# GpSimd takes over the last layer norm's centring and gamma, and the planner's leads and grain change, in a four-layer graph network on one core

## Chip, core and metric

The kernel runs on one core of a Trainium2 chip. The metric is device time in microseconds (us) of one execution. The engines are named as in the profile: PE (TensorE, matrix products), DVE (VectorE), ACT (ScalarE), POOL (GpSimd) and SP (its queue issues the DMAs).

## What is computed

Inputs are 32 batches of 256 nodes with 256 features, and one adjacency matrix. Four layers follow one another, each on a layer-normed copy of x and each added to x:

```python
h = relu(layernorm(x)); x = x + gnn(h)              # layer 0: degree * (own product + b) + adj @ (h @ Wj)
h = relu(layernorm(x)); x = x + gat(h)              # layer 1: one attention head, masked softmax
h = relu(layernorm(x)); x = x + attention(h)        # layer 2: q, k, v, 8 heads, output product
h = relu(layernorm(x)); x = x + gat_ffn(h)          # layer 3: 4 GAT heads, elu, output GAT, elu, ffn
# the end of layer 3:
y = ffn + out
return (y - mean(y)) / sqrt(var(y) + eps) * ln_gamma + ln_beta
```

The change touches the last line. There mean and variance are those of a row of y, 256 elements.

## The kernel before

A batch lies in SBUF as 128 partitions by 2 chunks (`C = 2`) by 256. The work of a batch is cut into 267 named steps, each with an engine, a planned cost and the steps that it needs. Names that come back below, for layer 1: `amj` (the last product of layer 0, L966 `ps<-wp,at`), `x1` (its sum into x, L1283), `stats 1`, `aggr 1` (L1246, L1252: mean and variance), `inv_std 1` (POOL, L722 to L727), `rows 1` (ACT, L806 `tb<-xs`: the normed rows), `rows_T 1` (PE, L995 `ps<-ident,tb`: four transposes into columns), `rows_hi 1` and `rows_lo 1` (L814 on ACT and L1260 on DVE into `hT1`: a value is kept as a high and a low part for exact products), and `wh 0` (PE, L966 `ps<-w1g,hT`: layer 1's product, a first part of 4 matmuls with high parts and 8 more that need the low part).

For the 8 heads of layer 2: `scores` (PE, L1160, two heads at a time), `smin` (DVE, L1408: two instructions and two short read-outs for each head), `s_exp` (ACT, L919), `p_T` (PE, L995 `ps<-ident,pb`), `pT16_hi` (ACT, L927), `pT16_lo` (DVE, L1416) and `values` (PE, L1177). For layer 3: `attend` (PE, `ps<-pT,whs`), `elu_relu`, `elu_exp` (ACT, L888, L892), `elu` (DVE, L1380), `join` (PE, `ps<-wout,hid`), `tmin 5` (DVE, L1343 into `tbo`), `out_b2` (POOL, L785). The last norm: `y` (DVE, L1434), `stats 4`, `aggr 4`, `y_gamma` (DVE, L1439), `inv_std 4` (POOL, two instructions), `final` (DVE, L1449) and `store`.

The order of the steps on every engine is fixed while the program is built, by a list planner (`arrange`): it keeps a planned time for each engine and takes again and again the ready step with the earliest planned start, rounded to `GRAIN`; among those with the same rounded start it takes the one with the longest rest of work behind it. To this rest, `LEAD` adds a constant by the section of the step: layers 0 and 1, layer 2, the rest of layer 3, and the ffn with the last norm. On the chip each engine then runs its list strictly in that order and waits on semaphores. So an instruction whose operands are late holds back all that stands behind it on its engine. Work of four batches is interleaved.

```python
start, st = min(((max(free[st["engine"]], st["ready"]), st) for st in ready),
                key=lambda of: (round(of[0] / GRAIN), -of[1]["rest"]))
```

Of the kernel before, what the change touches and what calls it, by code (L numbers as in the profile page):

```python
# [5 lines left out]
def adj_preln_kernel(nc, x, adj, adj_t, L0_W_t, L0_b, L1_W, L1_a_src, L1_a_dst,  # L6
# [33 lines left out]
    with ctx:  # L40
# [3 lines left out]
        def sem(name):  # L44
            return ctx.enter_context(nc.semaphore(name))
# [468 lines left out]
        def ffn(a):  # L514
            transposed(a, TR_OUT, ("elu", GOUT))
            a("out_b2", 0, PO, 1.37, ("rows_T", TR_OUT))
            a("ffn1", 0, TE, 1.4, ("rows_lo", TR_OUT))
            a("f1_full", 0, SC, 0.75, ("ffn1", 0))
            a("f1_hi", 0, SC, 0.54, ("f1_full", 0))
            a("f1_lo", 0, PO, 1.25, ("f1_hi", 0))  # L520
            product(a, "ffn2", 0, (("f1_hi", 0),), (("f1_lo", 0),))
            a("y", 0, VE, 0.6, ("ffn2", 0), ("out_b2", 0))
            norm_chain(a, 4, ("y", 0))
            a("y_gamma", 0, VE, 0.8, ("aggr", 4))
            a("final", 0, VE, 0.8, ("y_gamma", 0), ("inv_std", 4), ("x_beta", 0))
            a("store", 0, SY, 0.05, ("final", 0))

# [51 lines left out]
            assert len(order) == len(todo)  # L579
            return order  # L580

        GRAIN, LEAD = 0.2, (34.0, 34.0, 33.0, 33.0)
        ISSUE = (0.07, 0.04, 0.05, 0.05, 0.05)

        SECTIONS = (("load", "x_deg", "mj", "mi", "mj_hi", "mj_lo", "x_mi", "amj", "x1", "x2"),
# [84 lines left out]
        wo_done, normalised = sem("wo_done"), sem("normalised")  # L670
        f1_done, f1_full, f1_hi, f1_lo, f2_done = (sem(n) for n in ("f1_done", "f1_full", "f1_hi", "f1_lo", "f2_done"))
        ob_ready, y_done = sem("ob_ready"), sem("y_done")
        vstep = sem("vstep")

        def batch(t, b):
            return t[b].rearrange("(c p) d -> p c d", p=P)
# [1 line left out]
        def run_steps(block, order):  # L678
# [32 lines left out]
            def _(pool):  # L711
# [59 lines left out]
                def normalise(p, u):  # L771
# [7 lines left out]
                    else:  # L779
                        last.then_inc(normalised, 1)  # L780

                def out_b2(_, u):
                    pool.wait_ge(rows_T[TR_OUT], u + 1)
                    for c in range(C):
                        last = pool.tensor_tensor(fu5[:, c, :], fu5[:, c, :], b2_b[:], ALU.add)  # L785
                    last.then_inc(ob_ready, 1)

                program = dict(inv_std=inverse_std, x_deg=x_deg, scale=scale, v_c=value_third, x_bo=x_bo, x_beta=x_beta, hid_lo=low_of_hidden, out_b2=out_b2, normal=normalise, f1_lo=low_of_ffn)
                for name, k, u in order:
                    if name in program:  # L790
                        program[name](k, u)
# [428 lines left out]
            def _(dve):  # L1220
# [3 lines left out]
                def mark(ins, key):  # L1224

                    count[0] += 1
                    ins.then_inc(vstep, 1)
                    marks[key] = count[0]
# [204 lines left out]
                    dve.wait_ge(ob_ready, u + 1)  # L1433
                    dve.tensor_tensor(fu5[:], fu5[:], bank(BJ), ALU.add).then_inc(y_done, 1)  # L1434

                def times_gamma(_, u):
                    dve.wait_ge(mv_ready[4], u + 1)
                    for c in range(C):
                        last = dve.scalar_tensor_tensor(out=fu5[:, c, :], in0=fu5[:, c, :], scalar=mv[4][:, c, 0:1],  # L1439
                                                        in1=gamma_b[:], op0=ALU.subtract, op1=ALU.mult)  # L1440
                    mark(last, ("yg",))

                def result(_, u):
                    dve.wait_ge(rstd_ready[4], u + 1)
                    after(("yg",))
                    dve.wait_ge(beta_ready, u + 1)
                    xu = xs[u % XB]
                    for c in range(C):
                        last = dve.scalar_tensor_tensor(out=xu[:, c, :], in0=fu5[:, c, :], scalar=rstd[4][:, c:c + 1],  # L1449
                                                        in1=xu[:, c, :], op0=ALU.mult, op1=ALU.add)  # L1450
                    last.then_inc(x_final, 1)
# [44 lines left out]
```

## Time and profile before

| | |
|---|---|
| median of 3 runs | 1876.4 us (1875.9 to 1878.53) |
| the profiled execution, its own time | 1877.61 us |
| its span, first to last instruction | 1875.7 us |
| busy PE, DVE, ACT, POOL | 1746.8, 1573.2, 1539.7, 862.1 us |
| mean granted clock | 0.98 |

The span leaves out 1.9 us that lie around the first and the last instruction. "Busy" is the time in which at least one instruction of the engine ran. A busy PE may still lose some time between its matmuls. Instructions of one engine overlap slightly, by about 80 ns on DVE, so distances between starts are used below, not durations.

### The profile page before, as it was taken

Reading aid. Unit: us, or ns where it says so; the run is one execution under the profiler, and the core shown is the slowest. Engines: PE = TensorE matmul, PEld = TensorE weight load, DVE = VectorE, ACT = ScalarE, POOL = GpSimd, SP = SyncE. Lnnn points to the kernel's source line nnn. Section 1 sums busy time; section 2 is a strip of 40 time slices with the busy share of each in tenths; the row PEclk is TensorE's granted clock in tenths of the full one; section 3 lists DMA queues with packets and bytes.
Section 4 is the critical chain, followed back from the end, with each engine's and each line's share of the span. In section 5 each row is a group of like instructions: output and inputs, shape, how many; then the busy total and the mean of one; then the engine's idle time right before and its main releaser. Section 6 shows DMA issues by size and latency. Waiting matters only on the chain. (4 is left out here: it accounts for less than half of the span.)

```text
span 1875.7 us, 45892 instructions
## 1 busy us (share of the span) xinstructions
PE 1746.8 (93%) x15880; PEld 1661.5 (89%) x15880; DVE 1573.2 (84%) x5359; ACT 1539.7 (82%) x3634; POOL 862.1 (46%) x1492
## 2 busy tenths in 40 slices
PE   0789999999999999999999999999999999999985
PEld 0678999999999999999999999999999999999874
DVE  6478988888889888888998888889888889988863
ACT  2368988888899888888988888898888889888872
POOL 4224544445554444555444445544444554443442
PEclk8799999999999999999999999999999999999997
DMA  5000000000000000000000000000000000000000
GB/s 165 12 24 2 20 23 19 24 25 24 13 24 19 19 24 24 24 13 24 19 23 19 24 24 21 16 19 24 18 24 24 13 24 19 24 13 19 18 18 12
DMA packets 31206, 43.83 MB, mean 23 GB/s; under 512 B 3328, under 2 KB 26880, under 8 KB 30976
## 3 DMA queue, kind: packets, MB, share of 16 engines
q1 hardware_dynamic: 30976, 40.91, 6.7%
q8 instruction: 127, 2.08, 0.5%
q14 instruction: 103, 0.84, 0.2%
HBM read 32.38 MB, written 8.52 MB: 22 GB/s over the span
## 5 line engine op out<-in xcount | busy, mean ns | idle before, releaser
L775 POOL TENSOR_TENSOR cx<-cx,rden 128x64 f32<-128x64 f32 x256 | 78.3, 327 | 511.8 <-DVE cx L1426 511.8
L919 ACT ACTIVATE pb<-lg,hmin 128x256 f32<-128x256 f32 x512 | 227.1, 499 | 42.3 <-DVE hmin L1408 39.8
L966 PE MATMUL ps<-wout,hid 128*128 128x256 f32 x1536 | 228.7, 290 | 1.8 <-ACT hid L933 1.0
L927 ACT ACTIVATE pT<-ps 128x512 f16<-128x512 f32 x256 | 145.5, 590 | 97.9 <-PE ps L1177 92.7
L1408 DVE CUSTOM_DVE_ANT_0 lg<-ps,maskp 128x256 f32<-128x256 f32 x512 | 190.9, 419 | 26.9 <-PE ps L1160 24.7
L966 PE MATMUL ps<-wh,hT 128*128 128x256 f32 x1536 | 212.4, 288 | 0.8 <-DVE whs L1324 0.8
L966 PE MATMUL ps<-pT,whs 128*128 128x256 f32 x1536 | 206.0, 283 | 3.0 <-DVE pT L1373 1.9
L966 PEld LDWEIGHTS ps<-wout,hid 128*128 128x128 f32 x1536 | 196.3, 190 | 9.9 <-ACT hid L933 1.4
L765 POOL TENSOR_TENSOR hid<-fu,hid 128x512 fp32r<-128x512 f32 x128 | 166.7, 1303 | 76.8 <-ACT hid L933 76.8
L966 PEld LDWEIGHTS ps<-pT,whs 128*128 128x128 f32 x1536 | 192.4, 191 | 4.2 <-DVE pT L1373 2.5
L966 PEld LDWEIGHTS ps<-wh,hT 128*128 128x128 f32 x1536 | 191.2, 190 | 3.9 <-DVE whs L1324 1.3
L1416 DVE TENSOR_TENSOR pT<-ps,pT 128x512 f16<-128x512 f32 x256 | 170.7, 686 | 10.1 <-ACT pT L927 8.9
L745 POOL TENSOR_SCALAR ea<-ea,rs 128x256 f32<-128x256 f32 x256 | 132.2, 530 | 86.0 <-DVE rs L1364 85.3
L863 ACT ACTIVATE ea<-tb,npeak 128x256 f32<-128x256 f32 x320 | 161.4, 507 | 0.1
L849 ACT ACTIVATE tb<-tb,cols 128x256 f32<-128x256 f32 x320 | 145.2, 508 | 18.7 <-DVE dmin L1343 18.7
L995 PE MATMUL ps<-ident,pb 128*128 128x128 f32 x1024 | 148.3, 275 | 5.1 <-ACT pb L919 4.5
L1380 DVE SCALAR_TENSOR_TENSOR fu<-rb,ps 128x512 f32<-128x512 f32 x160 | 108.8, 680 | 44.5 <-ACT rb L892 38.3
L1177 PE MATMUL ps<-v,pT 128*128 128x97 bf16 x2048 | 130.1, 208 | 10.0 <-DVE pT L1416 9.8
L1177 PEld LDWEIGHTS ps<-v,pT 128*128 128x128 f16 x2048 | 106.3, 98 | 24.8 <-DVE pT L1416 16.8
L1160 PE MATMUL ps<-kp,qp 32*128 32x256 f32 x1536 | 124.8, 294 | 2.3 <-DVE kp L1387 0.4
L995 PEld LDWEIGHTS ps<-ident,pb 128*128 128x128 f32 x1024 | 117.1, 141 | 9.0 <-ACT pb L919 8.5
L723 POOL TENSOR_TENSOR rstd<-ve,pow_half 128x2 f32<-128x2 f32 x160 | 117.4, 734 | 13.3
(188 smaller groups left out, 4790.0 us busy)
## 6 DMA issues: line engine op xcount, KB each, us to landing
tbc<-t_dram SPq DMA_DIRECT2D x32, 512.0 KB, 3.7
xin<-x_in SPq DMA_DIRECT2D x32, 256.0 KB, 2.7
out<-xs SPq DMA_DIRECT2D x32, 256.0 KB, 2.2
t_dram<-st_rows SPq DMA_DIRECT2D x128, 1.0 KB
xs<-a_heads SPq DMA_DIRECT2D x4, 128.0 KB, 5.5
pT<-a_heads SPq DMA_DIRECT2D x4, 128.0 KB, 4.5
lg<-W_out SPq DMA_DIRECT2D x2, 256.0 KB, 5.2
tb<-adj SPq DMA_DIRECT2D x1, 256.0 KB, 2.8
```

Source lines behind the costliest of these rows:

```text
L745: last = pool.tensor_scalar(ea(g)[:, c, :], ea(g)[:, c, :], rs[g][:, c:c + 1], 1.0, ALU.mult, ALU.mult)
L765: pool.tensor_tensor(hid[g % 2][:, 1], fu[:], f(hid[g % 2][:, 0]), ALU.subtract).then_inc(hid_lo, 1)
L849: last = act.activation(tb(g)[:, c, :], tb(g)[:, c, :], ACT.Prelu, bias=source_cols(g)[:, c:c + 1], scale=-1.0, alpha=SLOPE[g])
L863: act.activation(ea(g)[:, c, :], tb(g)[:, c, :], ACT.Exp, bias=npeak[g][:, c:c + 1], scale=1.0, accum_out=psums[g][:, c:c + 1]).then_inc(e ...
L919: last = act.activation(pb[h % 2][:, c, :], lg[h % 2][:, c, :], ACT.Exp, bias=hmin[h % 2][:, c:c + 1], scale=-1.0)
L927: act.activation(pT16[h % 2][:, 0], bank(head_bank(h)), ACT.Copy).then_inc(pT16_hi, 1)
L966: last = pe.matmul(dst, lhs(a, t), rhs(b, t), start=(not low and opens and n == 1), stop=(low is not False and closes and n == terms * len ...
L995: last = pe.transpose(bank(k)[:, kc, blk(c)], src[:, c, blk(kc)], ident[:])
L1160: last = pe.matmul(bank(head_bank(h))[:, c, :], qp[r, a, oc, blk(c)], kp[r, b, oc, :], start=(n == 0), stop=(n == 2))
L1177: last = pe.matmul(ps[:, at0:at0 + VC], pT16[h % 2][:, part, kc, blk(c)], v3[:, kc, h, :], start=(n == 0), stop=(n == 2 * C - 1))
L1408: last = dve.tensor_tensor_reduce(out=lg[h % 2][:, c, :], in0=bank(head_bank(h))[:, c, :], in1=maskp[:, c, :], scale=-SCALE, scalar=3.0e38 ...
L1416: dve.tensor_tensor(pT16[h % 2][:, 1], bank(head_bank(h)), pT16[h % 2][:, 0], ALU.subtract)\
```

## The change

`y_gamma` moves from DVE, where it is two instructions (subtract the mean, times gamma), to POOL, where it is four: two that subtract the mean, each waited for by its own semaphore, and two that multiply by gamma. `final` on DVE now waits for a semaphore from POOL. The planner's cost of the step becomes 2.3 in place of 0.8. `GRAIN` goes from 0.2 to 0.1 and `LEAD` from (34, 34, 33, 33) to (21, 25, 18, 26). All engines' orders are planned anew.

```diff
-            a("y_gamma", 0, VE, 0.8, ("aggr", 4))
+            a("y_gamma", 0, PO, 2.3, ("aggr", 4))
...
-        GRAIN, LEAD = 0.2, (34.0, 34.0, 33.0, 33.0)
+        GRAIN, LEAD = 0.1, (21.0, 25.0, 18.0, 26.0)
...
-        vstep = sem("vstep")
+        vstep, y_gamma = sem("vstep"), sem("y_gamma")
...
+                def times_gamma(_, u):
+                    pool.wait_ge(mv_ready[4], u + 1)
+                    for c in range(C):
+                        made(pool.tensor_scalar(fu5[:, c, :], fu5[:, c, :], mv[4][:, c, 0:1], 1.0, ALU.subtract, ALU.mult))
+                    for c in range(C):
+                        last = pool.tensor_tensor(fu5[:, c, :], fu5[:, c, :], gamma_b[:], ALU.mult)
+                    last.then_inc(y_gamma, 1)
...
-                def times_gamma(_, u):
-                    dve.wait_ge(mv_ready[4], u + 1)
-                    for c in range(C):
-                        last = dve.scalar_tensor_tensor(out=fu5[:, c, :], in0=fu5[:, c, :], scalar=mv[4][:, c, 0:1],
-                                                        in1=gamma_b[:], op0=ALU.subtract, op1=ALU.mult)
-                    mark(last, ("yg",))
-
                 def result(_, u):
                     dve.wait_ge(rstd_ready[4], u + 1)
-                    after(("yg",))
+                    dve.wait_ge(y_gamma, u + 1)
```

Where the planner puts the rows is shown at three places of one period in the middle of the program. Line numbers of the new kernel are 8 higher from the inserted function on. "x8" counts like instructions in a row.

**Place 1**, layer 1's norm. DVE before: `x_mi`, `x1`, `stats 1`, a low part of layer 2, `aggr 1`, then `gather` of layer 2.

```order
L1275 SCALAR_TENSOR_TENSOR xs0<-ps,deg,xs0 128x256 x2
L1283 TENSOR_TENSOR xs0<-xs0,ps 128x512
L1246 BN_STATS stats1<-xs0 128x6 x2
L1416 TENSOR_TENSOR pT160<-ps,pT160 128x512
L1252 BN_AGGR mv1<-stats1 128x2 x2
L1424 RECIPROCAL rden<-ps 128x4
L1426 TENSOR_REDUCE cx<-ps 128x2x32 x2
```

The same place on DVE in the changed kernel (L1388 is `elu` of head 4, L1416 is `smin` of heads 4 and 5):

```order
L1388 SCALAR_TENSOR_TENSOR fu<-rb,ps 128x512
L1291 TENSOR_TENSOR xs0<-xs0,ps 128x512
L1254 BN_STATS stats1<-xs0 128x6 x2
L1416 ISA lg0,hmin0<-ps,maskp 128x256
L1416 ISA hmin0 128x1
L1416 ISA lg0,hmin0<-ps,maskp 128x256
L1416 ISA hmin0 128x1
L1416 ISA lg1,hmin1<-ps,maskp 128x256
L1416 ISA hmin1 128x1
L1416 ISA lg1,hmin1<-ps,maskp 128x256
L1416 ISA hmin1 128x1
L1260 BN_AGGR mv1<-stats1 128x2 x2
```

`elu` now stands ahead of `x1`, and `smin 4` and `smin 5`, which need the scores, stand between the statistics and `aggr 1`. On PE in the changed kernel the rows from the scores of heads 4 and 5 (L1168) to the transposes of layer 1's rows (`ident,tb1`) and on to the scores of heads 6 and 7 are:

```order
L1168 MATMUL ps<-kp,qp 128x256 x12
L974 MATMUL ps<-wout,hid0 128x256 x8
L974 MATMUL ps<-wout,hid1 128x256 x4
L1185 MATMUL ps<-v3,pT160 128x97 x8
L974 MATMUL ps<-wout,hid0 128x256 x4
L1003 MATMUL ps<-ident,pb0 128x128 x4
L1185 MATMUL ps<-v3,pT161 128x97 x8
L1003 MATMUL ps<-ident,pb1 128x128 x4
L1003 MATMUL ps<-ident,tb30 128x128 x4
L1003 MATMUL ps<-ident,tb1 128x128 x4
L1185 MATMUL ps<-v3,pT160 128x97 x8
L1168 MATMUL ps<-kp,qp 128x256 x12
```

Before, the scores of heads 4 and 5 stood right ahead of these transposes, with no row between.

**Place 2**, just behind it. ACT in the changed kernel: `rows 1` (L814 `tb1<-xs0`) stands between the high parts of heads 4 and 5 (L935). Before it stood ahead of the exponentials of both heads.

```order
L927 ACTIVATE pb0<-lg0,hmin0 128x256 x2
L927 ACTIVATE pb1<-lg1,hmin1 128x256 x2
L935 ACTIVATE pT160<-ps 128x512
L814 ACTIVATE tb1<-xs0,nmr,rstd 128x256 x2
L935 ACTIVATE pT161<-ps 128x512
L841 ACTIVATE who<-ps 128x512
```

DVE before: layer 1's low part (`hT1`) stands behind `smin 5` and ahead of `tmin 5` (`tbo`).

```order
L1408 ISA lg1,hmin1<-ps,maskp 128x256
L1408 ISA hmin1 128x1
L1260 SCALAR_TENSOR_TENSOR hT1<-ps,hT1 128x512
L1343 ISA tbo,dmin<-ps,mask3p 128x256
L1343 ISA dmin 128x1
```

DVE in the changed kernel, where `smin 6` (`lg0`), `tmin 5` and `smin 7` (`lg1`) have come ahead of it:

```order
L1416 ISA lg0,hmin0<-ps,maskp 128x256
L1416 ISA hmin0 128x1
L1351 ISA tbo,dmin<-ps,mask3p 128x256
L1351 ISA dmin 128x1
L1351 ISA tbo,dmin<-ps,mask3p 128x256
L1351 ISA dmin 128x1
L1416 ISA lg1,hmin1<-ps,maskp 128x256
L1416 ISA hmin1 128x1
L1416 ISA lg1,hmin1<-ps,maskp 128x256
L1416 ISA hmin1 128x1
L1268 SCALAR_TENSOR_TENSOR hT1<-ps,hT1 128x512
```

**Place 3**, the last norm on POOL in the changed kernel (L785 and L787 are the new step, L722 and L723 with `mv4` are `inv_std 4`):

```order
L745 TENSOR_SCALAR ea31<-ea31,rs 128x256 x2
L785 TENSOR_SCALAR fu5<-fu5,mv4 128x256 x2
L787 TENSOR_TENSOR fu5<-fu5,gamma_b 128x256 x2
L722 TENSOR_SCALAR ve<-mv4 128x2
L723 TENSOR_TENSOR rstd<-ve,pow_half 128x2
L765 TENSOR_TENSOR hid1<-fu,hid1 128x512
```

Before, `inv_std 4` followed the L745 rows directly, with `inv_std 0` behind it; now the new step is ahead of it, and a low part that the join of head 1 needs (`hid1`) is behind it.

## Rows read from the trace of the kernel before

**Rows 1.** Stretches: PE, PEld, DVE, ACT, POOL busy, PEclk, DMA share, GB/s.

```profile
180.00:1700.00 1520.00, 1495.65 (x13850) 1432.63 (x13850) 1338.66 (x4612) 1329.61 (x3159) 732.73 (x1281) 1.00 0.06 21
1140.04:1194.75 54.71, 53.58 (x499) 51.33 (x498) 47.53 (x167) 47.71 (x115) 26.45 (x46) 1.00 0.06 21
```

**Rows 2.** PE groups, 180 to 1700 us: busy, mean ns, idle before, releaser.

```profile
L1177 PE MATMUL ps<-v,pT 128*128 128x97 bf16 x1792 | 114.0, 208 | 6.8 <-DVE pT L1416 6.8
L995 PE MATMUL ps<-ident,tb 128*128 128x128 f32 x336 | 52.1, 277 | 0.8 <-ACT tb L806 0.8
```

**Rows 3.** PE in order of time, around layer 1's norm.

```profile
1154.39 0.97 PE L1160 MATMUL ps<-kp,qp 32*128 32x256 f32 x12
1155.30 0.74 PE L966 MATMUL ps<-wout,hid 128*128 128x256 f32 x4
...
1158.27 1.58 PE L966 MATMUL ps<-wp,at 128*128 128x256 f32 x12
1159.69 0.60 PE L995 MATMUL ps<-ident,pb 128*128 128x128 f32 x4
1160.12 0.51 PE L1177 MATMUL ps<-v,pT 128*128 128x97 bf16 x8
1160.45 1.19 PE L966 MATMUL ps<-wout,hid 128*128 128x256 f32 x8
...
1165.10 0.66 PE L995 MATMUL ps<-ident,tb 128*128 128x128 f32 x4
```

**Rows 4.** DVE, the same stretch, in order of time.

```profile
1155.41 0.42 DVE L1408 CUSTOM_DVE_ANT_0 lg<-ps,maskp 128x256 f32<-128x256 f32 x1 [0.41 <-PE ps L1160]
...
1156.11 0.68 DVE L1380 SCALAR_TENSOR_TENSOR fu<-rb,ps 128x512 f32<-128x512 f32 x1
...
1161.97 0.24 DVE L1252 BATCH_NORM_AGGREGATE mv<-stats 128x2 f32<-128x6 f32 x2
```

**Rows 5.** POOL and ACT, the same stretch, in order of time.

```profile
1162.30 0.23 POOL L722 TENSOR_SCALAR ve<-mv 128x2 f32<-128x2 f32 x1 [2.79 <-DVE mv L1252]
...
1163.95 1.09 ACT L806 ACTIVATE tb<-xs,nmr,rstd 128x256 f32<-128x256 f32 x2 [0.82 <-POOL nmr L727]
1164.95 0.58 ACT L814 ACTIVATE hT<-ps 128x512 fp32r<-128x512 f32 x1
...
1170.58 0.60 ACT L927 ACTIVATE pT<-ps 128x512 f16<-128x512 f32 x1
```

**Rows 6.** From layer 1's low part to the next scores, DVE and PE.

```profile
1168.13 0.69 DVE L1260 SCALAR_TENSOR_TENSOR hT<-ps,hT 128x512 fp32r<-128x512 f32 x1
1168.74 0.42 DVE L1343 CUSTOM_DVE_ANT_0 tbo<-ps,mask3p 128x256 f32<-128x256 f32 x1
...
1169.42 0.18 DVE L1424 RECIPROCAL rden<-ps 128x4 f32<-128x4 f32 x1
...
1171.21 0.69 DVE L1416 TENSOR_TENSOR pT<-ps,pT 128x512 f16<-128x512 f32 x1 [0.29 <-ACT pT L927]
1168.88 1.23 PE L966 MATMUL ps<-w1g,hT 128*128 128x258 f32 x8
...
1171.95 0.98 PE L1160 MATMUL ps<-kp,qp 32*128 32x256 f32 x12
```

**Rows 7.** POOL's nearest instructions to the new step, and DVE's `y_gamma`.

```profile
1147.04 0.94 POOL L745 TENSOR_SCALAR ea<-ea,rs 128x256 f32<-128x256 f32 x2 [0.58 <-DVE rs L1364]
1149.21 1.45 POOL L760 TENSOR_TENSOR xs<-xs,beta_b 128x256 f32<-128x256 f32 x2
1189.11 1.30 POOL L745 TENSOR_SCALAR ea<-ea,rs 128x256 f32<-128x256 f32 x2 [0.48 <-DVE rs L1364]
L1439 DVE SCALAR_TENSOR_TENSOR fu<-fu,mv,gamma_b 128x256 f32<-128x256 f32 x56 | 30.7, 588 | 0.6
```

**Rows 8.** The end of the program, in order of time.

```profile
1870.64 0.50 POOL L722 TENSOR_SCALAR ve<-mv 128x2 f32<-128x2 f32 x1 [3.51 <-DVE mv L1252]
...
1872.07 0.88 DVE L1449 SCALAR_TENSOR_TENSOR xs<-fu,rstd,xs 128x256 f32<-128x256 f32 x2 [0.60 <-POOL rstd L723]
```

More of the change, by code:

```diff
@@ L786, in out_b2 @@
                     last.then_inc(ob_ready, 1)
-                program = dict(inv_std=inverse_std, x_deg=x_deg, scale=scale, v_c=value_third, x_bo=x_bo, x_beta=x_beta, hid_lo=low_of_hidden, out_b2=out_b2, normal=normalise, f1_lo=low_of_ffn)
+                program = dict(inv_std=inverse_std, x_deg=x_deg, scale=scale, v_c=value_third, x_bo=x_bo, x_beta=x_beta, hid_lo=low_of_hidden, out_b2=out_b2, normal=normalise, f1_lo=low_of_ffn, y_gamma=times_gamma)
                 for name, k, u in order:
@@ L1459, in _ @@
                                pT16_lo=low_of_turned, gather=gather_values, x3=x_plus_context,
-                               y=ffn_sum, y_gamma=times_gamma, final=result)
+                               y=ffn_sum, final=result)
                 for name, k, u in order:
```

## The prediction, made before the changed kernel ran

> **What bounds the kernel now.** I read the stretches first, because a share of the whole span mixes filling, steady work and draining. From 180 to 1700 us PE is busy 1495.65 of 1520 us, with the clock at 1.00, its level of 2.4 GHz; DVE and ACT are busy 1338.66 and 1329.61, or 88% each, and POOL less than half [rows 1]. The second row of that group is one period: it runs from the second half of ffn2 of one batch to that of the next, 54.71 us, and 1520 us hold 27.8 of them. So PE bounds the steady part. All that an order of the rows can give back there is PE's idle time, 1520 - 1495.65 = 24.35 us, or 24.35 / 27.8 = 0.88 us in a period. Work taken from DVE gives nothing by itself: it must end a wait of PE.
>
> Then the groups of PE, for where these 0.88 us lie. The largest is `values`, which waits for DVE's low part `pT16_lo`, 6.8 us over the stretch, a quarter of a microsecond in a period. The transposes `ident,tb` of the normed rows wait 0.8 us in all, next to nothing [rows 2]. The rest is spread in small pieces. So the old order has PE's row arrive nearly level with the end of each chain. What a new order does to those chains decides the time.
>
> **DVE loses `y_gamma`.** Its two instructions take 30.7 us over 56, 28 batches, so 1.10 us a batch [rows 7]. They stand in the period some 20 us ahead of the `values` wait and DVE is idle between (0.41 us, for one, ahead of `smin` [rows 4]). I cost this at 0.
>
> **POOL gains it.** No row shows a subtraction of the mean over 256 columns on POOL; the nearest is the pair L745, 0.94 us, with one input and a column of scalars, and the two waits add about 0.08 us each, the distance of dependent POOL instructions. The multiplications by gamma are of the form of L760, 1.45 us for the pair [rows 7]. Sum 0.94 + 0.16 + 1.45 = 2.55 us; bounds are 2.4 (no waits) and 1.30 + 1.45 + 0.2 = 2.95 (the slow pair of L745). POOL is busy 26.45 of 54.71 us [rows 1], so there is room. Behind the new step stand `inv_std 4`, then the low part of head 1 for `join`. On DVE `final` waits now for 2.55 + 1.43 us after `aggr 4`, where 1.43 is from `ve` to `final` [rows 8], so 4.0 us. In the new order `k_lo`, `probs_lo`, `smin 0` and `smin 1` stand between. `smin 0` can't start before the scores, which wait for `k_lo`: 0.85 for `k_lo`, 0.74 to PE (as from L1416 to the scores [rows 6]), 1.02 from the scores to `smin` (1154.39 to 1155.41 [rows 3, 4]), and 1.40 for two heads (0.70 each, 1155.41 to 1156.11 [rows 4]) make 4.0. So the wait is level with what hides it, and I cost it at 0 in the steady part. If the cover is gone, `final` holds `v_r`, `probs_lo` and `elu` back by what is missing.
>
> In the last batch nothing hides it. There `ve` follows `aggr 4` at once and `final` starts 1.43 us later [rows 8]. With the new step ahead of `inv_std 4` on POOL this is 2.55 us more: **+2.6 us**, once.
>
> About contention: the L745 pair took 1.30 us, not 0.94, where it ran beside `tmin`, whose two inputs (`tbc`, `mask3p`) lie in SBUF; that is 0.36 us [rows 7]. Beside the new step stand `k_lo`, `probs_lo` and `smin`, which read one input from PSUM; I add nothing. The Trainium skill, page "SBUF — State Buffer", section "Who interferes with whom", says that a VectorE instruction with two SBUF inputs and a GpSimd instruction that reads SBUF exclude each other for a whole instruction. By it the new step costs DVE nothing beside PSUM readers, the same 0; where it met `tmin` it would speak against the change.
>
> **The new order, place 1.** Today the chain from `amj` to `rows_T 1` starts at 1158.27 and the transposes start at 1165.10, 6.83 us later, right when `rows 1` ends, with PE's work in between just as long [rows 3, 5]. In the new order `aggr 1` stands behind `smin 4` and `smin 5`, so the chain begins at the scores instead: 1.02 (scores to `smin`) + 1.40 (two heads) + 0.33 (`aggr` to `ve`, 1161.97 to 1162.30) + 1.65 (`ve` to `rows`, to 1163.95) + 1.15 (`rows` to the transposes, to 1165.10) = 5.55 us [rows 3 to 5]. PE has in this time the scores, 0.91 (1154.39 to 1155.30); 16 matmuls of `join` at 0.118 (`amj`: 12 in 1.42), 1.9; three times four transposes at 0.43, 1.3; and two `values` at 0.33 to 0.40, 0.8 [rows 3]. That is 4.9 us. PE waits about **0.6 us**, in every batch. `elu` of head 4 ahead of `x1` can only make it more.
>
> **Place 2, first part.** `rows 1` on ACT now stands between the high parts of heads 4 and 5. From its start: 1.00 until ACT takes the next (1163.95 to 1164.95 [rows 5]), 0.63 from high to low part (1170.58 to 1171.21 [rows 5, 6]), 0.74 until the scores (1171.95 [rows 6]), so 2.37 us. PE has the 1.15 until the transposes, these, 0.43, and one `values`, 0.40: 1.98. **0.4 us** more, in place of today's wait for the same low parts.
>
> **Second part.** Layer 1's low part now stands behind `smin 6`, `tmin 5`, `smin 7`. From the scores: 1.02 + 0.70 + 0.68 (`tmin`, 1168.74 to 1169.42) + 0.70 + 0.75 (low part to `wh 0`, 1168.13 to 1168.88) = 3.85 us [rows 4, 6]. PE's rows between are 12 scores, 4 matmuls of the spread, 6 + 4 of layers 3 and 1, one `values`, 4 transposes: 0.91 + 0.48 + 1.2 + 0.40 + 0.43 = 3.4. **0.4 us** more.
>
> Three places give 1.4 us a period. The other rows of the period moved too. Below they may cost nothing; above, as much again as these three, 1.4. I take 0.3, near the lower end, since at these three places a row of another chain now cuts a chain that PE waits for, and elsewhere the chains keep their shape. I let all of today's 0.88 us vanish, since PE now comes later to those places. Net (1.4 + 0.3 - 0.88) = 0.8 us in a period. Four batches fill and drain in almost the same rows as before, so I count 28 periods: 28 x 0.8 = 22 us, and with the end 25 us. The profiled execution took 1877.6 us, so 1902.6; the median of the runs shown is 1.2 lower, so **1901 us**.
>
> **Rivals.** The time of a change that measures as no change is within 0.2%, 3.8 us, of 1876.4, about what a measurement of this kernel can tell.
>
> *Waits overlap and the new order is faster.* My PE work at the three places is the least, from undisturbed distances. If small losses between groups stretch it by 0.3 to 0.4 us at each, the new waits shrink to about 0.4 in all; with 0.88 gone, the net is -0.48, times 28 = -13 us, +2.6: about 1866. For it speaks that the old order's period also holds far more than its idle time in such losses; against it, that the old chain and PE's work at place 1 agreed within 0.1 us when counted in the same way. It decides once the sum of the new waits is under 0.88. Chance 0.27.
>
> *It comes to nothing:* new and old waits are equal, 1873 to 1880. Chance 0.10.
>
> *POOL is the new wait.* `mv4` comes late, POOL stands at the new step, and the low part for `join 1`, 2.55 us later than in its old place, holds PE. Up to 1.3 us a period if a wait of that length is only half covered, 28 x 1.3 = 36, about 1915. Against it: PE takes that row some 9 us into the period. Chance 0.08.
>
> *Forecast:* slower by the three places, chance 0.55, its own range 1884 to 1928.
>
> **Range.** Lowest thinkable is all idle time gone and none new, 1876.4 - 24.6 + 2.6 = 1854; highest is 1.4 + 1.4 - 0.88 = 1.92 a period, 54 + 2.6 more, 1933. Cases of both signs hold much of the chance. I give 1862 to 1928. Slower: 0.55 + 0.08 = 0.63; same 0.10; faster 0.27.
>
> **What would show it.** In the new profile the transposes `ident,tb` on PE should wait for ACT's `tb` rows by about 0.6 us a batch, some 17 us over 28; the scores for `pT16_lo`, about 0.4; `ps<-w1g,hT` for DVE's `hT`, about 0.4. PE's busy time should stay at 1747, DVE's fall by 35 us, POOL's rise by 80. The period should be 55.5 us. At the end, `ve` should start about 2.6 us after `aggr 4`. The prediction is wrong if the period is below 54.7, which would mean that PE's work at the three places was longer than I counted, or that waits elsewhere, which I let vanish at the same price in any case, had held more than their idle time.

## The result and the profile after

The changed kernel takes 1949.85 us, the median of 4 runs (1947.28 to 1950.96), against 1877.47 for the kernel before, run beside it. The ratio is 1.037, 95% interval 1.035 to 1.0391. It is slower, as forecast, but by 72 us and not by 25: outside the range. Of all executions reported here one, of the kernel called e10 below, was in a slower state (2044.08 us at a granted clock of 0.83) and is not counted. The profiled execution took 1950.9 us, its span is 1949.3 us, and the mean granted clock 0.98.

The same stretch as in [rows 1], with its columns:

```profile
180.00:1700.00 1520.00, 1440.70 (x13292) 1371.46 (x13291) 1296.60 (x4385) 1274.61 (x3034) 786.43 (x1334) 1.00 0.06 20
```

PE is still the busiest, still at 2.4 GHz (1.00), but it now idles 1520 - 1440.70 = 79.3 us where it idled 24.35. The median distance from the ffn2 of one batch to that of the next, batches 6 to 24, went from 54.34 to 56.53 us (the period in [rows 1], 54.71, is one of the longer ones). 28 x 2.19 = 61 us of the 72 lie there. The rest isn't at the end alone: from the first `y` on DVE to the last, 31 distances, the changed kernel takes 71.9 us more (1723.7 against 1651.8), it reaches the first one 2.0 us earlier, and what follows the last takes 3.7 us more; so the batches of filling and draining slow down too. Idle time explains nearly all of it: 79.3 / 1520 x 56.53 - 24.35 / 1520 x 54.34 = 2.08 us a period.

The waits of PE in this stretch, instruction and what it waited for, then the sum in us, how often, and the longest:

```profile
PE ps L974 <- POOL hid L765: 30.8, 24, 1.4
PE ps L974 <- DVE fu L1388: 14.9, 24, 0.6
PE ps L1003 <- ACT tb L814: 11.6, 26, 0.8
PE ps L974 <- DVE hT L1268: 6.1, 26, 0.2
PE ps L1003 <- ACT cx L814: 3.7, 15, 0.4
```

The third and fourth are the forecast's places: `rows_T 1` waits for `rows 1`, 0.45 us a time, and `wh 0` for layer 1's low part, 0.23. The two ahead of them were not in the sum: `join 1` waits 1.28 us a time for POOL's low part `hid_lo 1`, and `attend 3` waits 0.62 for `elu 2` on DVE. Both stand behind the moved step. Seven smaller ones follow in the list, 8.8 us in all, among them a single wait of 2.7 us at 223. POOL, in order of time, in one period:

```profile
1186.95 0.94 POOL L745 TENSOR_SCALAR ea<-ea,rs 128x256 f32<-128x256 f32 x2
1187.87 2.40 POOL L785 TENSOR_SCALAR fu<-fu,mv 128x256 f32<-128x256 f32 x2
1190.35 1.44 POOL L787 TENSOR_TENSOR fu<-fu,gamma_b 128x256 f32<-128x256 f32 x2
1191.88 0.23 POOL L722 TENSOR_SCALAR ve<-mv 128x2 f32<-128x2 f32 x1
1192.19 0.72 POOL L723 TENSOR_TENSOR rstd<-ve,pow_half 128x2 f32<-128x2 f32 x1
1192.88 1.27 POOL L765 TENSOR_TENSOR hid<-fu,hid 128x512 fp32r<-128x512 f32 x1
1194.24 1.15 POOL L745 TENSOR_SCALAR ea<-ea,rs 128x256 f32<-128x256 f32 x2
```

The pair that subtracts the mean takes 2.40 us; the pair of L745, the row I had taken for it, takes 0.94 right above it. From the step's start to `ve` pass 4.01 us, not 2.55. POOL doesn't idle between these rows: `hid_lo 1` (L765) starts only when the step and `inv_std 4` are through. Nor does the step start when its input is there. DVE is through with `aggr 4` at 1186.67, and POOL, busy with the rows of `inv_std 0` and L745, takes the step up 1.2 us later:

```profile
1186.43 0.24 DVE L1260 BATCH_NORM_AGGREGATE mv<-stats 128x2 f32<-128x6 f32 x2
```

What ACT and PE did meanwhile:

```profile
1184.96 0.63 ACT L941 ACTIVATE hid<-fu 128x512 fp32r<-128x512 f32 x1
```

```profile
1191.72 1.04 PE L1003 MATMUL ps<-ident,pb 128*128 128x128 f32 x8
1194.20 0.73 PE L974 MATMUL ps<-wout,hid 128*128 128x256 f32 x4 [1.44 <-POOL hid L765]
1194.77 1.60 PE L974 MATMUL ps<-w,hT 128*128 128x256 f32 x12
1196.98 1.67 PE L974 MATMUL ps<-pT,whs 128*128 128x256 f32 x12 [0.61 <-DVE fu L1388]
```

The high part that `hid_lo 1` needs was ready at 1185.6, seven microseconds before POOL took it up. And DVE:

```profile
1190.41 0.42 DVE L1416 CUSTOM_DVE_ANT_0 lg<-ps,maskp 128x256 f32<-128x256 f32 x1
...
1192.94 2.10 DVE L1450 SCALAR_TENSOR_TENSOR xs<-fu,rstd,xs 128x256 f32<-128x256 f32 x2 [2.10 <-POOL rstd L723]
1194.97 0.68 DVE L1408 TENSOR_TENSOR cx<-ps,v 128x512 f32<-128x512 f32 x1
1195.57 0.68 DVE L1381 TENSOR_TENSOR pT<-ps,pT 128x512 fp32r<-128x512 f32 x1
1196.16 0.67 DVE L1388 SCALAR_TENSOR_TENSOR fu<-rb,ps 128x512 f32<-128x512 f32 x1
```

`final` (L1450) makes DVE idle 2.10 us for `inv_std 4`, and then takes 2.10 us itself. The idle time adds up: from the end of `aggr 4` it is 1.20 until POOL starts, 4.01 of step and 1.06 from `ve` to `final`, 6.27 us, against 4.17 that the rows between cover (to 1190.84). Behind it stand `v_r`, a `probs_lo`, and `elu 2` (L1388), for which `attend 3` waits. The groups of `final`, in the kernel before and in the changed one, over the same stretch:

```profile
L1449 DVE SCALAR_TENSOR_TENSOR xs<-fu,rstd,xs 128x256 f32<-128x256 f32 x56 | 24.3, 473 | 0.4 <-POOL rstd L723 0.4
```

```profile
L1450 DVE SCALAR_TENSOR_TENSOR xs<-fu,rstd,xs 128x256 f32<-128x256 f32 x52 | 53.5, 1067 | 50.9 <-POOL rstd L723 50.9
```

The same instruction takes 473 ns on average before and 1067 after. In the period above, the trace gives its two instructions by themselves:

```profile
L1450 DVE SCALAR_TENSOR_TENSOR xs<-fu,rstd,xs x2: 696/1087/1478, 1192.9 to 1194.3; 128x256 f32<-128x256 f32 x2
```

(durations min, median, max, then the starts of first and last). The first, 1478 ns, lies beside POOL's L765, the second beside L745. Both inputs of `final`, `fu` and `xs`, lie in SBUF. The Trainium skill, page "SBUF — State Buffer", section "Who interferes with whom", says that such an instruction and a GpSimd instruction that reads SBUF lock each other out for a whole instruction. The trace agrees in the main: 1478 ns is the 1.27 us of L765 and some 0.2 more, though a full wait and then the usual 473 ns would be 1.7.

At the end of the program, where [rows 8] stand for before:

```profile
1940.60 2.39 POOL L785 TENSOR_SCALAR fu<-fu,mv 128x256 f32<-128x256 f32 x2 [3.52 <-DVE mv L1260]
1943.08 1.40 POOL L787 TENSOR_TENSOR fu<-fu,gamma_b 128x256 f32<-128x256 f32 x2
1944.57 0.23 POOL L722 TENSOR_SCALAR ve<-mv 128x2 f32<-128x2 f32 x1
```

`ve` starts 3.97 us after `aggr 4` released POOL; forecast were 2.6 us.

### The profile page after: what moved, and what is told of

Its sections match the earlier page's. It is cut to its first block and busy times, and to the rows that moved or that the text cites. A ratio compares the mean times of both kernels' runs of the same rounds, so it can differ in the third digit from the quotient of the medians.

```text
span 1949.3 us, 45956 instructions
## 1 busy us (share of the span) xinstructions
PE 1756.4 (90%) x15880; PEld 1659.9 (85%) x15880; DVE 1579.1 (81%) x5295; ACT 1537.7 (79%) x3634; POOL 968.4 (50%) x1620
## 3 DMA queue, kind: packets, MB, share of 16 engines
q8 instruction: 127, 2.08, 0.5%
## 5 line engine op out<-in xcount | busy, mean ns | idle before, releaser
L927 ACT ACTIVATE pb<-lg,hmin 128x256 f32<-128x256 f32 x512 | 221.6, 499 | 93.9 <-DVE hmin L1416 91.0
L775 POOL TENSOR_TENSOR cx<-cx,rden 128x64 f32<-128x64 f32 x256 | 70.8, 297 | 350.9 <-DVE cx L1434 350.9
L745 POOL TENSOR_SCALAR ea<-ea,rs 128x256 f32<-128x256 f32 x256 | 129.6, 518 | 214.5 <-DVE rs L1372 211.6
L974 PE MATMUL ps<-pT,whs 128*128 128x256 f32 x1536 | 214.1, 289 | 16.4 <-DVE fu L1388 15.8
L765 POOL TENSOR_TENSOR hid<-fu,hid 128x512 fp32r<-128x512 f32 x128 | 164.3, 1284 | 119.5 <-ACT hid L941 119.5
L1416 DVE CUSTOM_DVE_ANT_0 lg<-ps,maskp 128x256 f32<-128x256 f32 x512 | 188.1, 419 | 30.9 <-PE ps L1168 30.6
L935 ACT ACTIVATE pT<-ps 128x512 f16<-128x512 f32 x256 | 146.2, 587 | 16.0 <-PE ps L1003 13.6
L941 ACT ACTIVATE hid<-fu 128x512 fp32r<-128x512 f32 x128 | 80.6, 630 | 90.4 <-DVE fu L1388 85.9
L1168 PE MATMUL ps<-kp,qp 32*128 32x256 f32 x1536 | 125.6, 295 | 4.3 <-DVE kp L1395 3.4
L896 ACT ACTIVATE rb<-ps 128x512 f32<-128x512 f32 x160 | 95.4, 596 | 40.8 <-PE ps L974 40.7
L1388 DVE SCALAR_TENSOR_TENSOR fu<-rb,ps 128x512 f32<-128x512 f32 x160 | 108.7, 679 | 22.8 <-ACT rb L900 17.0
L723 POOL TENSOR_TENSOR rstd<-ve,pow_half 128x2 f32<-128x2 f32 x160 | 115.0, 719 | 13.3
```

The source lines that it names most:

```text
L745: last = pool.tensor_scalar(ea(g)[:, c, :], ea(g)[:, c, :], rs[g][:, c:c + 1], 1.0, ALU.mult, ALU.mult)
L765: pool.tensor_tensor(hid[g % 2][:, 1], fu[:], f(hid[g % 2][:, 0]), ALU.subtract).then_inc(hid_lo, 1)
L927: last = act.activation(pb[h % 2][:, c, :], lg[h % 2][:, c, :], ACT.Exp, bias=hmin[h % 2][:, c:c + 1], scale=-1.0)
L935: act.activation(pT16[h % 2][:, 0], bank(head_bank(h)), ACT.Copy).then_inc(pT16_hi, 1)
L974: last = pe.matmul(dst, lhs(a, t), rhs(b, t), start=(not low and opens and n == 1), stop=(low is not False and closes and n == terms * len ...
L1168: last = pe.matmul(bank(head_bank(h))[:, c, :], qp[r, a, oc, blk(c)], kp[r, b, oc, :], start=(n == 0), stop=(n == 2))
```

## Experiments

All are timed against the kernel before, run on the same chip in the same session; its median was 1877.4 to 1882.3 us, so the ratio is the number to compare by. "Period" is the median over batches 6 to 24, "idle" that of PE from 180 to 1700 us.

| kernel | median us | ratio (95%) | period | idle | clock in the stretch |
|---|---|---|---|---|---|
| before | 1877.47 | 1 | 54.34 | 24.4 | 1.00 |
| changed | 1949.85 | 1.037 (1.035 to 1.0391) | 56.53 | 79.3 | 1.00 |
| e1 | 1904.84 | 1.0138 (1.0123 to 1.0153) | 55.22 | 54.7 | 1.00 |
| e2 | 2028.99 | 1.0799 (1.0781 to 1.0817) | 58.69 | 90.6 | 0.96 |
| e3 | 1970.73 | 1.0482 (1.0461 to 1.0504) | 57.45 | 82.4 | 0.99 |
| e4 | 2006.33 | 1.0674 (1.0642 to 1.0707) | 58.53 | 92.3 | 0.98 |
| e5 | 1945.33 | 1.0358 (1.0342 to 1.0373) | 56.27 | 74.3 | 1.00 |
| e6 | 1905.89 | 1.0148 (1.0133 to 1.0163) | 55.20 | 48.0 | 1.00 |
| e7 | 1930.24 | 1.0279 (1.0262 to 1.0297) | 55.70 | 66.2 | 1.00 |
| e8 | 1989.51 | 1.0591 (1.0575 to 1.0607) | 58.24 | 90.7 | 0.97 |
| e9 | 1904.14 | 1.0134 (1.0117 to 1.0152) | 55.12 | 53.9 | 1.00 |
| e10 | 2000.6 | 1.065 (1.063 to 1.0669) | 58.78 | 97.1 | 0.97 |
| e11 | 2000.01 | 1.064 (1.062 to 1.0659) | 58.79 | 99.3 | 0.97 |
| e12 | 1918.11 | 1.0194 (1.0179 to 1.0209) | 55.70 | 64.9 | 0.99 |
| e13 | 1899.32 | 1.0088 (1.0071 to 1.0105) | 54.89 | 46.1 | 1.00 |

e1, e6, e9, e12 and e13 are less than 2% slower than the kernel before, but no interval holds 1.

**e1: the new order without the new engine.** Every engine keeps the changed kernel's list; only `y_gamma`'s work is back on DVE, right ahead of `final` (a place that the planner didn't choose for DVE). The edit in DVE's part:

```diff
                 def result(_, u):
+                    times_gamma(_, u)
                     dve.wait_ge(rstd_ready[4], u + 1)
-                    dve.wait_ge(y_gamma, u + 1)
+                    after(("yg",))
```

> Planned exactly as the changed kernel (its leads, grain and cost 2.3 on POOL), but y_gamma runs on DVE, right ahead of final, and POOL has nothing in its place. Theory P (POOL's four instructions, 3.9 us, hold back the low part of head 1 and final, and with them join and attend 3: 1.33 + 0.71 us a period): the period falls from 56.55 to about 54.6 us, the time to 1885 to 1895 us, and those two waits of PE are gone. Theory O (the new order itself costs, by its cut chains at places 1 and 2): the time stays at 1935 to 1950 us.

It gave 1904.8 us, +27, where I had forecast 22 in the periods for the order. The rest of the 72, 45 us, is what it costs to have the step on POOL and not there on DVE; I had put that at 2.6. Between the two theories it lies near the first, but one of the two waits that were to go is still there. The waits of PE:

```profile
PE ps L966 <- DVE fu L1380: 20.7, 25, 0.9
PE ps L995 <- ACT tb L806: 11.9, 27, 0.8
PE ps L966 <- DVE hT L1260: 6.8, 27, 0.7
PE ps L995 <- ACT cx L806: 4.3, 16, 0.4
```

The places forecast are there (second and third), but the largest, `attend 3` for `elu 2`, is one that I had not looked at. It isn't the order's alone. Ahead of `elu 2` DVE now runs `y_gamma` as well, in 1.49 us in one period, and `final` behind it in 1.18:

```profile
1167.67 1.49 DVE L1439 SCALAR_TENSOR_TENSOR fu<-fu,mv,gamma_b 128x256 f32<-128x256 f32 x2
```

So the 27 us are the order together with `y_gamma` at this place on DVE; no run has the order by itself.

**e2: the new engine without the new order.** The lists of the kernel before; the four POOL instructions stand right ahead of `inv_std 4`, a place from which they delay nothing of POOL's that stood ahead of it. The edit in POOL's part:

```diff
                 def inverse_std(n, u):
+                    if n == 4:
+                        times_gamma(n, u)
```

> Planned exactly as the kernel before, but y_gamma's four instructions run on POOL, right ahead of inv_std 4, and final waits for them. Theory P: final and the rows behind it on DVE and POOL come 3 to 4 us later, 1 to 2 us a period, 1905 to 1935 us. Theory O: hidden but for the end of the program, 1880 to 1884 us.

2029 us, the slowest of all, and far above both theories (1935 at most). DVE waits in `final` for POOL 103.4 us over the stretch, up to 4.5 at a time, and PE behind it:

```profile
PE ps L976 <- DVE pT L1383: 53.3, 20, 3.3
PE ps L976 <- DVE fu L1390: 14.8, 5, 3.6
```

The old list has `final` close behind `aggr 4`, with an attention head's low part behind it. So the new order isn't the main loss; with the step on POOL it takes 79 us less than the old one. A part of these 79 is the clock, 0.96 in e2's stretch.

**e3 and e4: planner's numbers.** e3 is the kernel before with only `GRAIN` 0.1 and the new `LEAD`; e4 is the changed kernel with `GRAIN` 0.2 and the old `LEAD`. In both the planner makes lists that are in neither kernel. e3's edit:

```diff
-        GRAIN, LEAD = 0.2, (34.0, 34.0, 33.0, 33.0)
+        GRAIN, LEAD = 0.1, (21.0, 25.0, 18.0, 26.0)
```

> The kernel before with only grain 0.1 and leads (21, 25, 18, 26); the planner places y_gamma on DVE at cost 0.8. Theory P: 1870 to 1895 us. Theory O: 1930 us or more.

> The changed kernel with the old grain 0.2 and leads (34, 34, 33, 33); the planner places y_gamma on POOL at cost 2.3. Theory P: most of the loss is there, 1915 to 1950 us. Theory O: 1875 to 1890 us.

1970.7 and 2006.3 us: each half by itself is dearer than both together. e3 went as its second theory had it, e4 is beyond both. In e3 the idle time lies in many small waits (`values` 12.1, `attend` 11.5, the transposes of normed rows 11.2, `s_cols` 10.8, `join` 9.4 us), in e4 the largest is that of the scores for `pT16_lo`, 33.2 us, then that of the transposes for ACT's exponentials, 16.0. They say little on single causes, but this much: the parts of this change don't add.

**e5 and e6: the size of the POOL step.** e5 keeps the computation and writes the subtraction in two other forms; e6 multiplies by the mean where the changed kernel subtracts it, so it leaves out the centring and computes something else. First e5's edit, then e6's, both against the changed kernel.

```diff
-                    for c in range(C):
-                        made(pool.tensor_scalar(fu5[:, c, :], fu5[:, c, :], mv[4][:, c, 0:1], 1.0, ALU.subtract, ALU.mult))
+                    made(pool.tensor_scalar(fu5[:, 0, :], fu5[:, 0, :], 1.0, mv[4][:, 0, 0:1], ALU.mult, ALU.subtract))
+                    made(pool.tensor_scalar(fu5[:, 1, :], fu5[:, 1, :], mv[4][:, 1, 0:1], None, ALU.subtract))
```

> The changed kernel, but chunk 0's centring on POOL is (x times 1, minus mean) and chunk 1's is (x minus mean) with no second operation, where both were (x minus mean, times 1) at 1153 ns. Theory A (subtract is what is slow on POOL against the 487 ns of times-times): both stay near 1150 ns and the time near 1950 us. Theory B (it is the pair subtract-then-times that is slow): chunk 1 falls to 500 to 600 ns, perhaps chunk 0 too; the step to about 2.6 to 3.2 us and the time by 0.7 to 1.3 us a period, to 1915 to 1930 us.

```diff
-                        made(pool.tensor_scalar(fu5[:, c, :], fu5[:, c, :], mv[4][:, c, 0:1], 1.0, ALU.subtract, ALU.mult))
+                        made(pool.tensor_scalar(fu5[:, c, :], fu5[:, c, :], mv[4][:, c, 0:1], 1.0, ALU.mult, ALU.mult))
```

> The changed kernel, but POOL multiplies by the mean in place of subtracting it (the centring is left out). By the L745 rows of before it should take 487 ns in place of 1153, so the step 2.6 us, as was forecast for it. Theory Size (what went wrong is the 1.4 us that the step is longer than forecast): the wait of join and attend 3 falls by about 1.3 us a period, and the time to about 1912 us. Theory Place (standing ahead of head 1's low part and of final is dear at any size): above 1930 us.

The groups of these instructions, busy us, mean ns of one, idle before. In the changed kernel:

```profile
L785 POOL TENSOR_SCALAR fu<-fu,mv 128x256 f32<-128x256 f32 x54 | 62.2, 1153 | 3.0 <-DVE mv L1260 0.5
```

In e5, times 1 and minus the mean (L784), and minus the mean alone (L785):

```profile
L784 POOL TENSOR_SCALAR fu<-fu,mv 128x256 f32<-128x256 f32 x27 | 31.6, 1169 | 0.5 <-DVE mv L1260 0.5
L785 POOL TENSOR_SCALAR fu<-fu,mv 128x256 f32<-128x256 f32 x27 | 25.3, 938 | 2.5
```

In e6, two multiplications:

```profile
L785 POOL TENSOR_SCALAR fu<-fu,mv 128x256 f32<-128x256 f32 x54 | 26.0, 482 | 3.0 <-DVE mv L1260 0.5
```

Same shape, same operands, two operations each: 1153 with a subtraction, 482 without. (L745, the same form on other values, has a median of 487 before.) A single subtraction takes 938, so the second operation makes up a third of the difference. It isn't subtraction as such either: `hid_lo` (L765) subtracts one tensor from another, 128x512, in 1283 ns, 641 for 256 columns. What is slow here is the form that subtracts a column of scalars; an addition in this form was not tried. e5 took 1945.3 us, near the 1950 of the theory that subtraction is slow. From its start to `ve` the step now takes 2.68 us (1162.99 to 1165.67 in one period), about the length that I had forecast. With it e6 takes 1905.9 us, +28, and the wait of `join 1` is gone from the list of PE's waits; `attend 3` (15.5 us), `rows_T 1` (12.1) and `wh 0` (6.8) stay. So 44 of the step's 45 us hang on its length, and nearly all on one wait: PE's idle time falls by 31.3 us, from 79.3 to 48.0, and the wait of `join 1` was 30.8. On DVE `final` stays as slow as in the changed kernel, and DVE still waits for it, 16.1 us where it was 50.9:

```profile
L1450 DVE SCALAR_TENSOR_TENSOR xs<-fu,rstd,xs 128x256 f32<-128x256 f32 x54 | 56.1, 1077 | 16.1 <-POOL rstd L723 16.1
```

**e7: `final` behind `elu 2`.** The changed kernel; in 24 batches `final` on DVE comes right behind `elu 2` of the batch after.

```diff
-            run_steps(block, arrange())
+            run_steps(block, moved(arrange(), (("final", 0), ("elu", 2), 1, 60)))
```

(`moved` takes a step out of the list and puts it behind the other; 1 is the distance in batches.)

> The changed kernel, but final stands behind elu of head 2 on DVE, for 24 of the 32 batches, so it holds back neither the value's rest, nor probs_lo 3, nor elu 2. The wait of attend 3 (0.7 us a period) should go, and final leaves the company of POOL's hid_lo. Theory P: 24 x 0.6 = 14 us faster than the changed kernel, about 1935 us, with join's wait unchanged. If attend 3 only took over what join had left, no change.

1930.2 us, 20 less (expected were 14). `attend 3` waits no longer, `join 1` still does, 32.3 us; `final` takes 790 ns on average instead of 1067. So `final`'s place, with the wait and the slow instruction in it, has a price of its own. It isn't a part of the 44 us above: `attend 3` waits 14.9 us in the changed kernel and 15.5 in e6.

**e8: `hid_lo 1` first.** The changed kernel; on POOL `y_gamma` and `inv_std 4` come behind `hid_lo 1`.

```diff
-            run_steps(block, arrange())
+            run_steps(block, moved(arrange(), (("inv_std", 4), ("hid_lo", 1), 1, 60), (("y_gamma", 0), ("hid_lo", 1), 1, 60)))
```

> The changed kernel, but on POOL the low part of head 1 stands ahead of y_gamma and inv_std 4, for 24 of the 32 batches. Theory P: join's wait of 1.33 us a period goes, final comes 1.3 us later and attend 3 waits up to 1.3 us more, so between no change and 24 x 1.3 = 31 us faster than the changed kernel: 1918 to 1950 us.

1989.5 us, 40 more, where I had expected up to 31 less. The wait of `join 1` is gone (1.3 us in all), but `final` comes later and `attend 3` waits 56.6 us for `elu 2`, up to 2.6 at a time; the clock in the stretch falls to 0.97. POOL's 5 us of step and `inv_std 4` must lie ahead of one or the other.

**e9, e12: place 1.** e9 is e1 with `aggr 1` right behind the statistics. e12 is e9 with `rows 1` on ACT also moved, ahead of `pT16_hi 4`. The edit of e12 against e9:

```diff
-            run_steps(block, moved(arrange(), (("aggr", 1), ("stats", 1), 0, 60)))
+            run_steps(block, moved(arrange(), (("aggr", 1), ("stats", 1), 0, 60), (("rows", 1), ("s_exp", 5), -1, 60)))
```

> The new order with y_gamma on DVE (1904.8 us), but aggr 1 stands right behind stats 1, ahead of smin 4 and smin 5, for 24 batches. Theory Place 1: PE's wait for the tb rows (0.44 us a period) goes; 24 x 0.44 = 10 us faster, 1894 us. If another chain takes it over (the low part for the next scores), nothing or half.

> The kernel of e9 (the changed kernel's order with y_gamma on DVE, and aggr 1 right behind the statistics) with one step more moved, in 24 batches: rows 1 on ACT now stands behind the exponentials of head 5 and ahead of pT16_hi 4, no longer behind it. Theory A (place 1's wait is held by ACT's list: in e9 inv_std 1 ended at 1184.2 but rows 1 began at 1185.26, right behind pT16_hi 4, which waits for the transposes p_T 4): rows_T 1 no longer waits, 0.42 x 28 = 12 us less than e9's 1904, so about 1893. Theory B (there are two chains from the same scores, and ACT's row can serve only one of them first: pT16_hi 4 comes 0.5 to 1 us later, so values 4 on PE now waits for pT16_lo 4, by about 0.8 us where it waited 0.09): the wait moves from rows_T 1 to values 4 and the time stays at 1900 to 1915. I take B, 0.6 to 0.4.

e9 gave 1904.1 us, no change from e1, and `rows_T 1` waits as before. In e9, POOL, ACT and PE in one period:

```profile
1183.73 0.50 POOL L727 TENSOR_SCALAR nmr<-mv,rstd 128x1 f32<-128x1 f32 x2
```

```profile
1184.77 0.60 ACT L927 ACTIVATE pT<-ps 128x512 f16<-128x512 f32 x1
1185.26 1.08 ACT L806 ACTIVATE tb<-xs,nmr,rstd 128x256 f32<-128x256 f32 x2
```

```profile
1186.40 0.66 PE L995 MATMUL ps<-ident,tb 128*128 128x128 f32 x4 [0.42 <-ACT tb L806]
```

POOL is through with layer 1's norm at 1184.2, but `rows 1` starts only at 1185.26, right behind the high part of head 4 (L927), which stands ahead of it in ACT's list and waits for PE's transposes. The prediction's chain (`smin`, `aggr 1`, `ve`, `rows 1`) and this one (`smin`, exponential, `p_T 4`, high part, `rows 1`) end within 0.2 us of each other in e1, so taking one away gave nothing. In e12 both are cut, and the wait goes on: `rows_T 1` falls from 11.7 to 1.7 us, while `values 4` (L1177) now waits 25.2 for DVE's `gather` (L1426), which stands behind head 4's low part:

```profile
PE ps L1177 <- DVE cx L1426: 25.2, 22, 1.2
PE ps L966 <- DVE fu L1380: 20.2, 25, 0.9
```

1918 us, ratio 1.0194 against 1.0134: the wait moved, as the second theory had it, and at a price a little above its 1915. ACT can serve one of the two first, and the norm first is the dearer choice.

**e10, e11: the moves in e1's order.** e10 is e1 with `y_gamma` and `final` behind `elu 2`; e11 has that, e9's move, and layer 1's low part behind `smin 6`. The edit of e11 against e1:

```diff
-            run_steps(block, arrange())
+            run_steps(block, moved(arrange(), (("aggr", 1), ("stats", 1), 0, 60), (("final", 0), ("elu", 2), 1, 60), (("rows_lo", 1), ("smin", 6), 0, 60)))
```

> The new order with y_gamma on DVE, but y_gamma and final stand behind elu of head 2 on DVE, for 24 batches. PE's wait of attend 3 for elu 2 (0.77 us a period, the largest of this kernel) goes: 24 x 0.77 = 18 us faster, 1887 us. Against: the low parts of heads 0 and 1 behind it come later, and the gain is half.

> The new order with y_gamma on DVE and three moves on DVE for 24 batches: aggr 1 behind stats 1, final behind elu 2, and layer 1's low part ahead of tmin 5. PE's three largest waits (0.77, 0.44 and 0.25 us a period) go: up to 24 x 1.46 = 35 us faster than 1904.8, so 1870 us, and faster than the kernel before. If they only pass on to other chains: 1885 us or more.

The move that won 20 us in e7 loses 96 here, where I had expected 18 less. In e10, DVE, then PE:

```profile
1046.44 0.88 DVE L1439 SCALAR_TENSOR_TENSOR fu<-fu,mv,gamma_b 128x256 f32<-128x256 f32 x2
1047.41 2.74 DVE L1450 SCALAR_TENSOR_TENSOR xs<-fu,rstd,xs 128x256 f32<-128x256 f32 x2
1050.07 1.27 DVE L1416 TENSOR_TENSOR pT<-ps,pT 128x512 f16<-128x512 f32 x2
```

```profile
1046.83 1.59 PE L966 MATMUL ps<-pT,whs 128*128 128x256 f32 x12
1051.40 1.65 PE L1160 MATMUL ps<-kp,qp 32*128 32x256 f32 x12 [2.98 <-DVE pT L1416]
```

`final` takes 2.74 us. From 1047.30 to 1049.8 POOL runs `hid_lo 2` and `v_c`, 1.29 and 1.33 us long, which also read SBUF, and the two instructions of `final` take 1.36 and 1.46 us, about as long as those beside them. The low parts come 3 us late for the scores. What follows on PE, in stretches of 3 us with the columns of [rows 1]:

```profile
1045.00:1048.00 3.00, 3.00 (x27) 3.00 (x27) 2.67 (x5) 3.00 (x7) 0.70 (x1) 1.00 0.00 0
1048.00:1051.00 3.00, 0.42 (x4) 0.21 (x2) 3.00 (x4) 1.45 (x3) 3.00 (x3) 0.98 0.00 0
1051.00:1054.00 3.00, 2.60 (x17) 2.38 (x18) 1.85 (x7) 0.00 (x0) 1.55 (x2) 0.50 0.27 90
1054.00:1057.00 3.00, 3.00 (x26) 2.91 (x26) 1.76 (x6) 2.71 (x6) 0.09 (x1) 0.50 0.37 93
1057.00:1060.00 3.00, 3.00 (x25) 3.00 (x24) 2.09 (x6) 0.70 (x2) 1.69 (x3) 0.88 0.00 0
```

After the idle stretch the clock stands at 0.50, 1.2 GHz, for two stretches and part of a third. The twelve scores take 1.65 us there; they take 0.97 in [rows 3]. The time lost is thus the wait and, behind it, work at half the clock. The Trainium skill, page "TensorE: Matmul & The Clock Gate", Part 1, has these same two levels and a fall after idle time; the trace agrees with that much. e11's other two moves change nothing: 2000 us, and of the 35 us that were to be won at most nothing came.

**e13: e6 and e7 together.** The changed kernel with the multiplication by the mean and `final` behind `elu 2`.

> The changed kernel with two edits together: POOL multiplies by the mean in place of subtracting it (the centring is left out, so the step takes about 2.6 us and not 3.9), and final on DVE stands behind elu 2 in 24 batches. Apart they gave 1906 (e6) and 1930 (e7) against 1950. Theory A (the two prices are separate: join 1 behind POOL's long step, and attend 3 behind final and elu 2): e6's wait of attend 3, 15.5 us over the stretch, goes too, so about 1906 - 16 = 1890, and a period of 54.7. Theory B (what e7 won was only its part of the long step, and the shorter step already has it): 1902 to 1906.

1899.3 us, ratio 1.0088 against e6's 1.0148: 11 us less by the ratios, of the 16 that the wait of `attend 3` held in e6; it lies between the two theories. `attend 3` waits no longer, but the scores of heads 2 and 3, behind `final` now, wait 12.8 us for `pT16_lo`.

No version beats the kernel before, not even e13.

## Why the prediction was right or wrong

**What bounds the kernel: right.** PE bounds before and after, and the change acts through PE's waits. But the sign "DVE's fall by 35 us" failed: DVE is busy 1579.1 us where it was 1573.2, since `final` grew by about what `y_gamma` had taken. POOL rose by 106 us, not 80, and PE's busy time by 10, from 1746.8 to 1756.4.

**Place 1: the size was right, the cause half right.** The chain from the scores to `rows_T 1` took 5.60 us (1206.93 to 1212.53 in the changed kernel; forecast 5.55), the wait is 0.45 us a time (forecast 0.6). But e9 showed that a second chain through ACT's list is as long, and e12 that removing both makes it worse.

**Place 2: half.** The first part, scores for low parts, 0.4 forecast, isn't there: 0.6 us over the whole stretch. The second, `wh 0`, is: 0.23 for 0.4.

**The order as a whole: near in the sum, but by luck.** Forecast net +0.8 a period; e1 measures 55.22 - 54.34 = 0.88 (the 55.5 of the forecast started from the long period in [rows 1]). The places I had worked out give 0.44 + 0.25 in e1 (11.9 / 27 and 6.8 / 27), not 1.4; `attend 3`, 20.7 / 25 = 0.83 a time, fills the gap, and the sum had for all other places only 0.3. This wait hangs on what DVE does for the last norm ahead of `elu 2`, in e1 with `y_gamma` there, and not on the chains that the prediction cut at places 1 and 2.

**POOL's step: this failed.** The sum had "0.94 + 0.16 + 1.45 = 2.55 us", with bounds of 2.4 and 2.95. Measured is 2.40 + 1.44 and two small gaps, 4.01 to the next start: above the upper bound. The error is in one term, the row that stood for the subtraction: L745 multiplies twice, and the prediction took its shape and its operands for what sets the time. The nearest row by form was not the nearest by operation, and the bound was made from that same row beside a busy neighbour.

**"I cost it at 0 in the steady part": this failed too.** The argument had 4.0 us of wait against 4.0 of cover. Measured in one period are 6.27 against 4.17, so DVE waits 2.10 us in `final`. Of this, 1.46 is the length of the step. Another 1.20 is POOL's late start, which the sum left out: it let the step begin as soon as `aggr 4` was through, with POOL's rows of `inv_std 0` and L745 still ahead of it. (From `ve` to `final` it is 0.37 less than forecast, and the cover 0.17 more.) So "level" would have failed with a step of 2.6 us as well: e6 has 0.6 us of this wait each time, and PE's wait in `attend 3`, 15.5 us over the stretch. The text named what then stands behind `final` (`v_r`, `probs_lo`, `elu`) and gave it no price; e7 prices it at 20 us.

The larger part came on the other engine. Behind the step on POOL the low part for `join 1` is late as the rival "POOL is the new wait" described it: 1.28 us a time, where that rival had 1.3. It got a chance of 0.08 because PE takes that row "some 9 us into the period", with no time of POOL's to compare. POOL was through with it at 1194.15 and PE could have taken it at 1192.76; with a step 1.46 us shorter the two meet, and in e6 this wait is gone. Forecast and rival happened together: 1901 is nearly e1 and e6; this rival's 36 us on top gives 1937.

**Contention: "I add nothing" looked at the wrong instruction.** The rule was applied to what stands beside the new step, and there it held. But the order also sets `final` beside `hid_lo 1`, since both stand behind `inv_std 4`, and `final` is the DVE instruction with two SBUF inputs: 473 to 1067 ns, 1.2 us a batch. e6 has it too (1077 ns), so it is no part of the 44 us; it belongs to the wait of `attend 3`, and no run prices it apart from `final`'s place.

**The end:** 3.97 us for 2.6, the same error.

What stays open: the period of e1 and of the changed kernel also holds differences in how closely the matmuls follow one another, which no run separates; the order's own share, without any of `y_gamma` ahead of `elu 2`, was not measured; the loss in the batches of filling and draining is not located; and e3's and e4's losses are located but not explained. A form of the centring on POOL that is both exact and as fast as the multiplication wasn't tried.

## What to carry to other kernels

When work moves to an engine whose trace has no row for the operation, a row of the same shape is not a price; here the operation in the same form more than doubled it. Even the slowest row of this shape before (L760, about 0.73 us an instruction) would have bounded the step at 1.45 + 1.45 + 0.2 = 3.1 us, short of the 4.01 measured. So measure the instruction first, or let a rival stand for a longer one. And ask when the engine is free for the moved step, not only when its input is ready. A wait that is "level with its cover" is not worth 0: price what is queued behind it on both engines, the one that does the work and the one that waits. And where a list order puts an instruction with two SBUF inputs right behind the same release as a GpSimd instruction, count both in a row, not side by side.

## What the runs showed of the hardware

- A GpSimd `tensor_scalar` over 128x256 fp32 took 482 ns as two multiplications, 938 as one subtraction, 1153 to 1169 with a subtraction and a multiplication in either order.
- DVE's `final`, 473 ns by itself, took 1478 beside a GpSimd instruction of 1.27 us, and its pair took 2.74 us beside two of 1.29 and 1.33 us.
- `tensor_tensor` on GpSimd took 742 ns as a multiplication of 128x256 fp32 and 1283 as a subtraction of 128x512: there the subtraction was not the slower one.
- PE's granted clock fell behind waits. After one of 2.98 us it stood at 0.50 for some 6 us (e10), in most periods, and in the kernels with recurring waits of 2.6 to 3.6 us (e2, e8, e10, e11) the mean over the steady stretch was 0.96 to 0.97. In the changed kernel recurring waits of up to 1.4 us left it at 1.00, and its one wait of 2.7 us was followed by such a fall. But the length of a single wait does not decide it: e4 has none over 1.5 us and a mean of 0.98, and in e12 (0.99) this followed a wait of 1.24 us (1085.1 to 1086.4):

```profile
1089.00:1092.00 3.00, 3.00 (x21) 2.90 (x20) 2.49 (x14) 2.52 (x7) 0.00 (x0) 0.51 0.01 3
```
